# A Mamba block between two mixtures of experts on one core: the order of work inside a pipelined tile

## What is computed

```python
x = x + 0.5 * ffn(layernorm(x))      # 8 experts, top 2, 256 -> 512 -> 256, relu squared
x = x + mamba(layernorm(x))          # below
x = x + 0.5 * ffn(layernorm(x))
```

```python
u = layernorm(x)*ln_w + ln_b;  u = u @ W_in          # z | xBC | dt
dt = softplus(u_dt + dt_bias)
xBC = silu(conv4(u_xBC) + conv_b)                    # xs | B | C
h_t = h_(t-1) * exp(dt_t*A) + dt_t * x_t (x) B_t     # per head, 8 x 16
y_t = h_t . C_t + D * x_t
g = y * silu(z);  g = g * rsqrt(mean(g*g) + eps) * rms_w
out = x + g @ W_out
```

## Time and profile before

| what | value |
|---|---|
| median of 3 runs | 1264.49 us (1264.06 to 1264.54) |
| the profiled execution, its own time | 1263.04 us |
| its span, first to last instruction | 1261.0 us |
| instructions | 40440 |
| TensorE clock granted, mean over the span | 0.919 of full speed |
| Mamba layer, tiles 0 to 31 | about 369 us to 915 us of the span |

### The profile page before, as it was taken

How to read it: one execution, slowest core, us unless ns; L and a number is a source line. 1 busy time by engine, 2 the same in 40 slices (tenths; PEclk the granted TensorE clock), 3 DMA queues, 4 the chain that set the end, 5 groups by cost and what they waited for, 6 DMA issues and landing times.

```text
span 1261.0 us, 40440 instructions
## 1 busy us (share of the span) xinstructions
PE 990.8 (79%) x14528; PEld 857.0 (68%) x14528; DVE 942.7 (75%) x3006; ACT 681.9 (54%) x1586; POOL 544.8 (43%) x593
## 2 busy tenths in 40 slices
PE   3442799999479999999999999998664349999970
PEld 3441799999467777777777777776454349899960
DVE  4977466666379999999999999999377636666658
ACT  2332456655357777777777777776221125565640
POOL 2787133333323444544544445443258733333330
PEclk9999999999779999999999999999655569999985
DMA  9556344444336655666666566654312344444449
GB/s 233 179 189 205 75 99 103 102 100 103 101 64 114 117 107 105 115 110 114 116 111 119 106 109 114 107 104 83 64 51 89 117 100 95 99 100 101 103 113 359
DMA packets 194530, 148.05 MB, mean 117 GB/s; under 512 B 113952, under 2 KB 162080, under 8 KB 194208
## 3 DMA queue, kind: packets, MB, share of 16 engines
q0 software_dynamic: 41088, 70.49, 26.6%
q1 hardware_dynamic: 147488, 69.72, 23.3%
q10 hardware_dynamic: 5760, 5.26, 1.3%
HBM read 41.34 MB, written 51.61 MB: 74 GB/s over the span
## 4 chain that ended last, share of the span: by engine, by line
PE 54%; DVE 11%; issue 9%; POOL 9%; DMA 7%; SPq 7%; ACT 3%; POOLq 0%; DVEq 0%; ACTq 0%
PE bank L656 12%; PE bank L670 12%; PE bank L1225 9%; POOL disp L555 7%; PE bank L1294 4%; PE bank L1265 4%; SPq L606 3%; PE bank L1336 2%; PE bank L1361 2%; PE bank L1355 2%; DVE cv L864 2%; DMA disp<-arena,sloti 1%; PE bank L1273 1%; DMA X<-yg 1%; SPq L608 1%
## 5 line engine op out<-in xcount | busy, mean ns | idle before, releaser
L656 PE MATMUL bank<-arena,weights 128*128 128x128 f16 x3456 | 220.3, 221 | 57.6 <-DMA arena<-disp 56.8
L615 POOL DMA_INDIRECT ychosen<-arena,didx x144 | 140.0, 972 | 269.3 <-DVE didx L721 232.5
L656 PEld LDWEIGHTS bank<-arena,weights 128*128 x3456 | 207.8, 99 | 63.7 <-issue 60.8
L729 DVE TENSOR_TENSOR arena<-arena 128x512 f32<-128x512 f32 x144 | 99.7, 692 | 153.6 <-ACT arena L691 153.6
L670 PE MATMUL bank<-weights,arena 128*128 x1728 | 211.5, 273 | 0.0
L691 ACT ACTIVATE arena<-bank 128x512 f32<-128x512 f32 x144 | 86.0, 597 | 189.0 <-PE bank L656 174.6
L670 PEld LDWEIGHTS bank<-weights,arena 128*128 128x128 f16 x1728 | 163.1, 98 | 16.5
L555 POOL DMA_INDIRECT disp<-arena,sloti x128 | 133.7, 1045 | 58.9 <-issue 35.5
L864 DVE SCALAR_TENSOR_TENSOR cv<-U,vec,cv 128x128 f32<-128x128 f32 x480 | 128.6, 343 | 0.0
L1005 POOL DMA_DIRECT2D X<-yg x64 | 64.5, 1008 | 111.6 <-DMA X<-yg 104.9
L734 DVE TENSOR_TENSOR arena<-arena 128x512 f16<-128x512 f32 x144 | 99.6, 692 | 4.9
(11 more groups left out here) (165 smaller groups left out, 2169.7 us busy)
## 6 DMA issues: line engine op xcount, KB each, us to landing
arena<-in_w SPq DMA_DIRECT2D x16, 512.0 KB, 4.9
yg<-ychosen SPq DMA_DIRECT2D x32, 256.0 KB, 2.8
X<-yg POOLq DMA_DIRECT2D x64, 128.0 KB, 3.8
arena<-dtx SPq DMA_DIRECT2D x128, 64.0 KB, 3.2
yi<-yc POOLq DMA_DIRECT2D x32, 256.0 KB, 4.0
turned_y<-y SPq DMA_DIRECT2D x128, 64.0 KB, 1.8
yi<-turned_y POOLq DMA_DIRECT2D x32, 256.0 KB, 4.1
arena<-ychosen SPq DMA_DIRECT2D x32, 256.0 KB, 5.3
```

Source lines behind the costliest of these rows:

```text
L615: pool.indirect_dma_start(ychosen, bass.IndirectOffsetOnAxis(ap=didx[:, t % NIDX:t % NIDX + 1], axis=0), ysb[t % YB][:, :], None).then_inc ...
L656: mm = pe.matmul(o, chunk(where, 2 * ("hl".index(w) * WN + c * HID + m * P), P), v, start=c == 0 and n_ == 0, stop=c == KD - 1 and n_ == 2)
L729: dve.tensor_tensor(hq[t % 2][:, :], hr[t % 2][:, :], hr[t % 2][:, :], ALU.mult).then_inc(S("hq"), 1)
```

## The change

It changes the order of calls in the loops of four engines, moves the output of the squares to another buffer, and adds the waits that this needs. No operation is added or removed. TensorE does `turned_norm` and `intra` of tile i first, then `turned_gate` of tile i-1, `project_steps`, and only then `project_out` of tile i-1. VectorE does all four `decays` and `norm` before `gate`. ScalarE copies the state before `choices`, and does `squares` and `turned_gate` behind `out_of_heads`. POOL issues `add_state` directly behind `add_carried`, ahead of `add_choice` and `deviation`, and does `rms` ahead of the second `add_choice`.

```diff
 def weighted(k):                                     # VectorE
     dve.wait_ge(S("m_ee"), k + 1)
+    after(dve, "m_ss", k - 1)
     dve.wait_ge(S("m_dtx"), k + 1)
...
 def gate(k):                                         # VectorE
     dve.wait_ge(S("m_gz"), k + 1)
+    after(dve, "m_GTp", k)
+    after(dve, "m_ss", k)
     dve.tensor_tensor(G[:, :], yi[p][:, :], gz[p][:, :], ALU.mult).then_inc(S("m_G"), 1)
...
 # loop of VectorE
                     decays(i, 0)
-                if inside(i - 1):
-                    gate(i - 1)
-                if inside(i):
                     decays(i, 1)
                 if inside(i + 2):
                     norm(i + 2)
                 if inside(i):
                     decays(i, 2)
                     decays(i, 3)
+                if inside(i - 1):
+                    gate(i - 1)
                 if inside(i + 1):
                     conv(i + 1)
...
 # loop of POOL
                     add_carried(i)
+                    add_state(i)
                 if inside(i + 3):
                     add_choice(i + 3, 0)
                 if inside(i + 2):
                     deviation(i + 2)
+                if inside(i - 1):
+                    rms(i - 1)
                 if inside(i + 3):
                     add_choice(i + 3, 1)
-                if inside(i):
-                    add_state(i)
-                if inside(i - 1):
-                    rms(i - 1)
                 if inside(i):
                     add_turned(i)
...
 def squares(k):                                      # ScalarE
     act.wait_ge(S("m_G"), k + 1)
-    act.activation(tz[:, :], G[:, :], ACT.Square, accum_out=mss[:, 0:1]).then_inc(S("m_ss"), 1)
+    act.wait_ge(S("m_sp"), min(k + 2, NT))
+    act.activation(dtxw[:, :], G[:, :], ACT.Square, accum_out=mss[:, 0:1]).then_inc(S("m_ss"), 1)
...
 def gate_in(k):                                      # ScalarE
     act.wait_ge(S("m_z"), k + 1)
-    after(act, "m_ss", k)
     after(act, "m_gz", k)
...
 # loop of ScalarE
                     decays(i, 0)
                     decays(i, 1)
-                if inside(i + 4):
-                    choices(i + 4)
-                if inside(i):
                     state(i)
                     decays(i, 2)
                     decays(i, 3)
-                if inside(i - 1):
-                    squares(i - 1)
-                    turned_gate(i - 1)
+                if inside(i + 4):
+                    choices(i + 4)
                 if inside(i):
                     gate_in(i)
...
                 if inside(i):
                     out_of_heads(i)
+                if inside(i - 1):
+                    squares(i - 1)
+                    turned_gate(i - 1)
                 if inside(i + 1):
                     tanh_conv(i + 1)
...
 # loop of TensorE
                     gate_in(i)
-                if inside(i - 1):
-                    turned_gate(i - 1)
-                    project_out(i - 1)
                 if inside(i + 2):
                     turned_norm(i + 2)
                 if inside(i):
                     intra(i)
+                if inside(i - 1):
+                    turned_gate(i - 1)
                 if inside(i + 2):
                     project_steps(i + 2)
+                if inside(i - 1):
+                    project_out(i - 1)
+                if inside(i + 2):
                     project_bc(i + 2)
                     project_in(i + 2)
```

## The result

The changed kernel takes 1339.47 us (median of 4 runs, 1338.62 to 1341.65), the one before 1264.51: a ratio of 1.058, interval 1.056 to 1.060. It is 75 us slower, where 46 were forecast; the time lies inside the range.

A forecast was written before the change was run, and what follows sets the result against it. VectorE's list, 16.58 us a tile, was taken as the bound, TensorE within a microsecond. 29 tiles x 1.8 + 0.9 - 6.4 = +46.7 on 1263.0 gave 1309.7, stated as 1310 us; range 1284 to 1345.

The forecast's parts named there:

- The stall on POOL: On POOL `add_state` and the DMAs behind it delay the power to t = 5.2; VectorE's `norm` waits 1.58 us a tile.
- the cheap-POOL rival: POOL's DMAs cost only 0.54 us each in a row: stall 0.8, about 17.55 us a tile, 1286 us; chance 0.10.
- 18.4 us a tile by way of TensorE: Late `intra` on TensorE delays y1, squares, the copy GT and `project_out`: next L899 at 18.4, +1.8 us a tile.
- TensorE's clock: Rival: TensorE's clock halves after idle time, +2.4 us a fall; 1381 us in every tile, 1333 in a third; chance 0.15.
- The prediction's own sign of being wrong: Wrong if `norm` shows no wait on the power, or L899's spacing is below 17, or above 19 with clock below 1.
- The cover of the second `add_choice`, of `load` and `add_turned`: POOL's second `add_choice`, issued near t = 12.3, lands before its reader with 1 us to spare; `load` and `add_turned` are covered.
- The ends: Last Mamba tiles: tile 29 +0.9 us, tile 30 -3.4, tile 31's y1 sooner by 3.0; the last two together -6.4.
- The two rivals without the stall: Both suppose POOL's power ends before t = 3.66, so `norm` does not wait; chance 0.04 each.
- No change: Rival: POOL isn't late, `intra` starts at 5.46, `inter` ends at 16.8; +1 us, 1266 us; chance 0.04.
- Faster: Rival: POOL isn't late, TensorE bounds and `project_steps` covers the GT copy; each tile loses 0.5, 1243 us; chance 0.04.
- The Trainium skill's rule: Two-input VectorE and GpSimd instructions on SBUF block each other; the power, unheld, takes 0.56 not 0.76: 6 us less.

## Why the prediction was right or wrong

- **The stall on POOL: right, to the tenth.** hn ready at 2.47 (measured 2.46), `add_state` at 2.77 (2.76), power at 5.2 (5.22 in most tiles), `norm` waiting 1.58 (1.51). The two runs around POOL's order show it as the cause: without it the loss falls from 5.8% to 0.6 to 0.9%, alone it makes 2.1%. The two don't add up to 5.8: the rest needs both, the wait on POOL and a TensorE order that has nothing to do during it. One sentence of the step was wrong: `choices` on ScalarE had nothing to do with it. And the DMAs are done one behind the other, 0.88 us apart (said 0.86), as their ends say and not their starts: the cheap-POOL rival is out.
- **18.4 us a tile by way of TensorE: right** for the tiles with full clock (18.25). The wait for GT in such a tile was 0.51, as said.
- **TensorE's clock: the step that failed.** The forecast took "1.8 is less than 2.2, and full-clock work lies around it" and so 1.00 for the whole layer, and gave the fall 0.15. It fell in 17 of 29 tiles, after two gaps of 0.83 and 0.98 with 0.44 of work between them. The price of one fall was forecast as 2.4 us: it was 0.8 where the half clock lasted 3.4 us and 2.5 where it lasted 6.8. The rival's 1333 "in a third of the tiles" came nearest. This term, put at nothing in the sum, is with TensorE's stops the 32 us that the tiles took beyond 18.25; the sum missed the measured +75 by 29.
- **The range held by luck.** It allowed for a fallen clock in up to half the tiles at 2.4 us each. The clock fell in more than half of them; at 2.4 us each, 17 falls on top of 1310 would have made 1351, outside the range. They cost 1.9 on average, stops included, and the two errors offset each other. The prediction's own sign of being wrong, a spacing above 19 with a clock below 1, did come: 19.36. And the last addition slips: 1309.7 and 1.5 make 1311, not 1310.
- **The cover of the second `add_choice`, of `load` and `add_turned`: right.** `rms` was held until the convolution's end and POOL issues the second one at t = 12.3, as said, and VectorE waits for no DMA into X.
- **The ends: right in size.** Tile 29 +0.8 (said +0.9), tile 30 -2.9 (-3.4), the last gate -3.5 against its L899 (-3.0). TensorE's wait for the silu in tile 30 fell from 2.23 to 0.47. The 4.6 us ahead of tile 0 and 2.5 behind the last gate lie where no call was moved.
- **The two rivals without the stall.** "No change" had the undisturbed tile right (16.74) but left out two things: by starting `intra` at 5.46 it took `bd` for there, and `norm`, reached 0.6 earlier, meets the power that is late in some tiles. "Faster" assumed that TensorE bounds; with `project_out` later alone nothing was gained, so it doesn't.
- **The Trainium skill's rule (SBUF — State Buffer, Who interferes with whom)** gave 6 us less, as the power wouldn't be held behind VectorE. The power ended at 5.22, 0.02 from what the sum had with 0.76: here the row decides, and the 6 us were not there. But this is no test of the rule. The 0.56 was the length of L979, which works on one column (128x1), and the power of `norm` works on two (128x2); with VectorE idle it took 0.75, so the 0.76 can be its own length and not a hold.

## What to carry to other kernels

A call moved forward on an in-order queue brings its wait with it: count what stands behind it, and for which engine that is due, before counting what the moved call gains. Work that becomes ready earlier asks for its inputs earlier: a transfer that was in time while its reader started at t = 8.15 was late in 6 and 7 of 29 tiles when the reader was ready at 5.63. And idle time in two short pieces, under 1 us each, can be followed by the half clock on TensorE; fill it or keep other work beside it, and reorder only where the order was seen to cost, here the last two tiles.

## What the runs showed of the hardware that was not expected

- Two gaps of 0.83 and 0.98 us in 2.3 us of TensorE's time were followed by 3.4 us or more at half clock in 17 of 29 tiles, and not in 12 others with the same gaps. With 13 matmuls of 256 columns in them, the clock fell in 4 of 29 tiles in each of two runs, in seven of the eight beside a stop of 2.1 to 2.4 us.
- Two DMAs that POOL issues back to back start 0.54 apart in the profile and end 0.86 to 0.88 apart; the ends count.
- Four DMAs of 64 KB from SyncE, the last issued at t = 1.65, had all landed at t = 5.16 (median) with a DMA of 256 KB issued by POOL at t = 1.24, and at 4.08 with that one issued at 3.67.
- TensorE stops for up to 2.7 us inside a run of 128 small matmuls or a few matmuls behind it, mostly in the same tiles in each run of one kernel and in others in another kernel; the half clock often follows. What holds it is not shown.
